# A graph convolution on one core: SP fetches 44 gathered rows in a turn in place of 32

## The reference, cut to what matters

```python
h = relu(layernorm(x))                       # x: 12500 nodes x 128
xp = h @ lin1_w
C = 0.5 * (cos(edge_weight * PI / CUTOFF) + 1.0)
W = (ssp(edge_attr @ mlp_w1 + mlp_b1) @ mlp_w2 + mlp_b2) * C[:, None]   # 212500 edges, 50 -> 128
msg = xp[src] * W                            # gather of 212500 rows of xp
agg = segment_sum(msg, dst, num_segments=12500)      # dst is sorted
out = x + (ssp(agg @ lin2_w + lin2_b) @ lin_w + lin_b)
```

## Time and profile before

| | |
|---|---|
| median of 3 runs | 2022.07 us (2021.86 to 2024.72) |
| the profiled execution | 2022.45 us, its span 2020.7 us |
| busy: PE, DVE, ACT, POOL | 66%, 52%, 39%, 75% of the span |
| POOL's gathers in the main part | 1542, 944 ns each |
| rows fetched one by one | 3092 by SP, 3840 by ACT |
| granted TensorE clock, mean | 0.819 |

### The profile page before, as it was taken

One profiled execution on the slowest core, in us unless ns is written; L12 is line 12 of the kernel. 1 busy time (PEld: TensorE's weight loads), 2 busy tenths in 40 slices (PEclk: granted clock), 3 DMA queues, 4 the chain that ended last, 5 costly groups with the idle time before them and its releaser, 6 DMA issues.

```text
span 2020.7 us, 48993 instructions
## 1 busy us (share of the span) xinstructions
PE 1341.8 (66%) x12880; PEld 1108.7 (55%) x12881; DVE 1048.1 (52%) x3153; ACT 792.7 (39%) x925; POOL 1517.5 (75%) x1611
## 2 busy tenths in 40 slices
PE   5577667776776777676666666666666666666666
PEld 5465556655555556555555555555555555555454
DVE  8664655555545555555544444444544444445454
ACT  5764333333434443433343333333333334333332
POOL 7777777777777777777777777777777777777775
PEclk9887888888888878888787888778877878887887
DMA  9633343333343344334333233333333333333322
GB/s 320 247 94 92 89 97 88 98 98 92 92 99 97 88 97 99 87 93 102 87 88 97 77 97 90 84 98 81 92 94 80 98 86 88 97 88 87 96 76 51
DMA packets 114579, 202.33 MB, mean 100 GB/s; under 512 B 36409, under 2 KB 69917, under 8 KB 114173
## 3 DMA queue, kind: packets, MB, share of 16 engines
q0 software_dynamic: 51392, 105.35, 21.6%
q1 hardware_dynamic: 55228, 91.86, 14.7%
q10 hardware_dynamic: 7680, 1.98, 0.7%
HBM read 186.25 MB, written 12.80 MB: 99 GB/s over the span
## 4 chain that ended last, share of the span: by engine, by line
POOL 38%; ACTq 19%; issue 18%; ACT 16%; PE 4%; DVE 3%; DMA 1%; DVEq 0%; SPq 0%; POOLq 0%
POOL XG L460 38%; ACTq L576 17%; ACT TB L593 5%; ACT TB L587 4%; ACT TB L590 4%; ACTq L565 1%; PE PW L878 1%; ACT XG L482 1%; DMA XG<-xp_scratch,IX 1%; PE PA L897 1%; DVE XG L776 1%; DVE TB L651 1%; DVE SCR L630 1%; PE PX L824 1%; PE PX L862 0%
## 5 line engine op out<-in xcount | busy, mean ns | idle before, releaser
L460 POOL DMA_INDIRECT XG<-xp_scratch,IX x1542 | 1455.6, 944 | 470.6 <-issue 463.0
L776 DVE SCALAR_TENSOR_TENSOR XG<-PW,CC,XG 128x128 f32<-128x128 f32 x1602 | 453.1, 344 | 435.3 <-DMA XG<-xp_scratch,IX 399.6
L587 ACT ACTIVATE TB<-PX 128x1024 f32<-128x1024 f32 x208 | 212.8, 1023 | 1039.8 <-PE PX L862 532.9
L875 PE MATMUL PW<-BPB,ones 128*128 128x512 bf16 x415 | 183.7, 443 | 563.3 <-DVE XG L776 558.8
L878 PEld LDWEIGHTS PW<-W,TB 128*128 128x128 f32 x3314 | 545.9, 234 | 20.0
L878 PE MATMUL PW<-W,TB 128*128 128x128 f32 x3314 | 548.9, 320 | 0.0
L731 DVE SCALAR_TENSOR_TENSOR TB<-PX,TB 128x1024 f32<-128x1024 f32 x208 | 254.2, 1222 | 347.1 <-ACT TB L593 336.5
L875 PEld LDWEIGHTS PW<-BPB,ones 128*128 128x128 bf16 x415 | 41.2, 99 | 674.2 <-issue 670.2
L897 PE MATMUL PA<-OH,XG 128*64 128x64 f32 x6408 | 296.1, 259 | 0.0
L897 PEld LDWEIGHTS PA<-OH,XG 128*64 128x64 f32 x6408 | 265.4, 171 | 31.3 <-issue 18.4
L862 PE MATMUL PX<-AT,W 51*128 51x256 f32 x1662 | 258.2, 432 | 2.6 <-ACT XG L482 2.6
(11 more groups left out here) (107 smaller groups left out, 538.1 us busy)
## 6 DMA issues: line engine op xcount, KB each, us to landing
HA<-xp_scratch ACTq DMA_DIRECT2D x3840, 0.5 KB
AT<-attr_b SPq DMA_DIRECT2D x104, 512.0 KB
HT<-xp_scratch SPq DMA_DIRECT2D x3092, 0.5 KB
XG<-xp_scratch,IX POOLq DMA_INDIRECT x1542, 2.7
AG<-zero SPq DMA_DIRECT2D x1, 6400.0 KB, 21.6
xp_scratch<-XG SPq DMA_DIRECT2D x24, 256.0 KB
XR<-x SPq DMA_DIRECT2D x24, 256.0 KB
out<-XR SPq DMA_DIRECT2D x24, 256.0 KB, 3.8
```

Source lines behind the costliest of these rows:

```text
L460: e.indirect_dma_start(XG[q % XG_N][0:p, k * D:(k + 1) * D], None, xp, bass.IndirectOffsetOnAxis(ap=IX[0:p, t0 + k:t0 + k + 1], axis=0)).t ...
L587: e.activation(T, PXP[pair % 2][:, :], ACT.Abs).then_inc(s_ab, 1)
L776: ins = e.scalar_tensor_tensor(out=G, in0=weights(q)[0:p, k * D:(k + 1) * D], scalar=CC[0:p, t0 + k:t0 + k + 1], in1=G, op0=ALU.mult, op1= ...
L875: e.matmul(P[0:p, 0:n * D], ones[:, 0:p], BP[0][:, 0:n * D], start=True, stop=False, skip_group_check=True)
```

## The change

SP's turn gets 44 rows in place of 32. `HQ` has 34 quads in place of 25, spaced 12 quads, at times 8: 30, 42, 54, ..., 126, 138, 146, 158, ..., 402, 414. Tile `j`'s last row comes in turn ceil(128(j + 1)/44) - 1 and its quad is 18 + 4 ceil(128(j + 1)/44). POOL skips the first tile of each of these quads, so it has 9 gathers less. The row numbers lie in a table `SI` by turns (101 x 44 in place of 25 x 128), a turn is two halves, and a half loads 22 numbers with one instruction and then issues 22 rows; a wait for a free `HT` buffer stands between rows where a tile begins. The last row, number 4243, falls into turn 96 as its twentieth. ACT's rows, the buffers and the rest of SP's queue are as before.

```diff
-ROWS = 32
-NH = (NCH - 3 - 2) * ROWS // TILE
-HQ = {18 + (j + 1) * TILE * CHQ // ROWS: j for j in range(NH) if 18 + (j + 1) * TILE * CHQ // ROWS < NQ - 2}
+ROWS = 44
+TURNS = NCH - 3
+HQ = {18 + -(-(j + 1) * TILE // ROWS) * CHQ: j for j in range((TURNS - 2) * ROWS // TILE)}
+HQ = {q: j for q, j in HQ.items() if q < NQ - 2}
...
-        SI = sb("SI", [NH, TILE], i32)
+        SI = sb("SI", [TURNS, ROWS], i32)
...
-            def fetch(a, b):
-                n = a
-                while n < b:
-                    j, p = n // TILE, n % TILE
-                    m = min(8 - n % 8, b - n)
-                    if p == 0 and j >= HT_N:
-                        e.wait_ge(s_sc, HAND[j - HT_N] + 1)
+            def fetch(turn):
+
+                for h in range(0, ROWS, ROWS // 2):
+                    n0 = turn * ROWS + h
+                    if n0 >= END:
+                        return
                     _, at = nc.values_load_multi_w_load_instructions(
-                        SI[j:j + 1, p:p + m], engines=[mybir.EngineType.SP], min_val=0, max_val=ROW * (NODES - 1),
+                        SI[turn:turn + 1, h:h + ROWS // 2], engines=[mybir.EngineType.SP], min_val=0, max_val=ROW * (NODES - 1),
                     skip_runtime_bounds_check_because="src holds node numbers, which are below NODES")
-                    for i, v in enumerate(at):
-                        e.dma_start(HT[j % HT_N][p + i:p + i + 1, :].bitcast(u8), row(v)).then_inc(s_r[j % HT_N], 16)
-                    n += m
+                    for n, v in zip(range(n0, END), at):
+                        j, p = n // TILE, n % TILE
+                        if p == 0 and j >= HT_N:
+                            e.wait_ge(s_sc, HAND[j - HT_N] + 1)
+                        e.dma_start(HT[j % HT_N][p:p + 1, :].bitcast(u8), row(v)).then_inc(s_r[j % HT_N], 16)
...
-                fetch(min(END, (k - AT_N) * ROWS), min(END, (k - AT_N + 1) * ROWS))
+                fetch(k - AT_N)
...
-        "src_h": _np.ascontiguousarray(tiles(g["src"]).T[[quad(q)[0] for q in HAND]]),
+        "src_h": turns(tiles(g["src"]).T[[quad(q)[0] for q in HAND]], TURNS, ROWS),
```

## The result

| | before | after |
|---|---|---|
| median | 2023.39 us (4 runs, three of them those of the section on the time before) | 2340.71 us (2336.47 to 2343.56, 4 runs) |
| ratio, 95% interval | | 1.156 (1.154 to 1.159) |
| span of the profiled execution | 2020.7 us | 2339.5 us |
| POOL's gathers | 1542 | 1533 |

The forecast was 2010.9 us within a range of 2008.5 to 2037; the change costs 317 us. POOL has its 9 gathers less, and it does not matter.

What follows compares the result with a forecast made beforehand. POOL, gathering without a pause, was taken to bound the kernel: 9 gathers fewer at 1.249 us save 11.2 us, so span 2020.7 - 11.2 = 2009.5 us, plus 1.4 for the median, 2010.9 us; range 2008.5 to 2037.

Steps and rivals of the forecast that it cites:

- SP's part: what a turn costs after: SP's queue: twelve rows more add 3.96 us, loads take off 0.17, restarts 0.14; a turn goes from 14.56 to 18.2 us.
- rival (a): SP's queue becomes the bound because its turn is dearer than worked out, from 18.34 us a turn; chance 0.29 past break-even.
- strictly by number: Upper bound for SP's load of 22: 22/8 x 0.792 = 2.18 us, giving 2127 us; chance 0.03.
- The turn of 24 us: SP's turn if registers cost about 200 ns each, two loads of 22 making 8.8 us; set aside for the trace's prices.
- The two slopes: Register loads' price for each further number: 0.049 us on SP (one to eight), 0.053 on ACT (one to twenty).
- The sum over turns: SP's path to the end: 249.3 us plus 96 turns; at 18.2 us a turn it ends at 1996.5 us.
- POOL's 9 gathers: POOL loses 9 gathers at 1.249 us each, 11.2 us, all on the path that sets the end.
- The floor: POOL working without a pause sets the end: span 2009.5 us, median 2010.9 us; chance 0.57.
- Twelve rows at 0.33 us: SP's twelve additional single rows in a turn, each 0.33 us, together 3.96 us more.
- The dear first row behind a load: SP's first row after each load of 22 might cost 0.2 us more; turn 18.6 us, 2035 us, chance 0.12.
- The load of `x` rows: In SP's queue behind the longer turn; its sum comes out some 5 us earlier than the chunk's, so it decides nothing.
- Rival (c): The 9 gathers bring nothing because POOL fills its ring instead; alone it would give 2021 us; chance 0.01.

## Why the prediction was wrong

**The step that failed** is "SP's part: what a turn costs after", and in it the load of 22 numbers, taken at 1.50 us within 1.48 to 2.18. It measured 1.88 us at the start of the table's row and 4.88 at byte 88. Both loads together were 6.76 us a turn in place of 3.00. The mechanism by which that decides was forecast, as rival (a), with a chance of 0.29: SP's queue becomes the bound, chunks come late. Only its upper end, 2127 us, was too low, since the bound "strictly by number" took the price per number from loads of eight at multiples of 32 bytes (0.099 us), not from one that begins off a multiple of 16 (0.22 us). The turn of 24 us that the prediction set aside would have made 249.3 + 96 x 24 = 2553 us, for only one of the two loads is that dear.

**What the trace of before could have said.** The two slopes rested on counts of 1, 8 and 20, and on starts at bytes 0, 32, 64, ... for SP and 0 and 80 for ACT. No load of it began off a multiple of 16 bytes or ended off one, save those of one number. I looked at the count as the only thing that changes; the change also moved the start to a place unlike all others. The Trainium skill, "Runtime: NRT & Kernel Launch", section "Instruction fetch mechanics", gives about 200 ns for each register even in bulk. I set it aside because the page speaks of loads from HBM, and eight numbers took 0.79 us. From SBUF it fits the load off the 16 bytes (0.22 us a number) and each number of a rest (0.21); for loads of whole fours that begin on them it is two to three times too high (0.79 / 8 = 0.10, 1.97 / 28 = 0.07).

**The sum over turns** comes out near, by two errors that cancel in part. With the turn of the first four, 249.3 + 96 x 21.72 = 2334 us; the span is 2339.5. But the mean turn was 22.21 us, 0.22 of it stores and `x` loads, so 21.99: 0.27 more in each, 26 us in all. And the stretch behind turn 96 was taken at 102 us and took 80: its nine pairs went at 6.1 us, not 8.51. ACT's last row was issued at 2244.7 us and POOL's last gather at 2252.5, before this stretch begins (2259.3); which of the two frees the pairs, no run took apart. PE's first matrices of the last pair began at 2317.5, 22.0 us before the end (21.6 forecast).

```profile
2262.87 2.08 PE L864 MATMUL PX<-AT,W 51*128 51x256 f32 x8 [9.48 <-DMA AT<-attr_b]
...
2317.49 1.13 PE L864 MATMUL PX<-AT,W 51*128 51x20 f32 x6
```

**Point by point.** POOL's 9 gathers: right, 1533 of 944 ns; the 11.2 us were lost in its waits. The floor is real: the kernels with 36 and 40 rows, and the one with ACT's share cut, sit within 1.3 us of theirs. Twelve rows at 0.33 us: right in the kernel after (0.332), wrong near the limit of 4.4 rows a us. This is a second term put at nothing: rows of SP and ACT in one DMA engine. With aligned loads it would still have been 2064 us, outside the range. The dear first row behind a load: it stayed at 0.27 us behind 22 numbers, this risk was none. The load of `x` rows "decides nothing": DVE waited 200 us for it, 21 times, in an SP-bound kernel in which the chunks are as late, and with loads of 24 and 20 it stood on the chain that ended last; no run took it apart from the chunks. Rival (c), a full ring of POOL: it came, 282.6 us of waits, as a consequence of (a), as the forecast put it.

## What to carry to other kernels

A load of many registers from a table was priced here by where it begins and by its count's rest, 0.25 us for four numbers against 0.21 for one of a rest; cut tables so that every load begins at a multiple of four numbers and has a multiple of four. Before work is moved to a queue with reserve, sum that queue's turn, multiply its error by the number of turns (96 here: 0.1 us is 10 us), and ask of each instruction whether its start and size are like one that the trace has priced. And count what all queues send to the same place: two queues of single-row transfers, each within its own pace, were over a limit here that neither shows, and they delayed a share of every bulk load. Look at when the packets start, not only at when they are issued.

## What the runs showed of the hardware

- TENSOR_LOAD on SP from SBUF: 1.23 us for 16 numbers, 0.25 more for each four, 0.21 for each of a rest of one to three; 4.88 us for 22 numbers at six of eight starts, 1.92 at the two that are multiples of 16 bytes.
- Single rows of 512 bytes issued by SP and ACT together passed at 4.34 to 4.40 a us on average over 96 turns, in five kernels with different turns, beside this kernel's gathers and chunk loads. Near that limit an ACT row's packet started 5 to 12 us after its issue (median) in place of 1.2, and SP's rows were issued up to 0.35 us apart in place of 0.332.
- Near it, a sixteenth of every 512 KB chunk load (8 of 128 packets) started from 10.5 us after the issue on (median), the others within 3.3, and those packets took turns with the rows: all single rows go through one DMA engine (the kernel with loads of 24 and 20).
- In two sessions the unchanged kernel took 2827 and 2832 us, against 2023 in the others, with SP and ACT often halting at the same moments for 0.7 us. The chip of the first has the same number, 3, as that of a later session with 2023 us, so it is not shown that the chip is the cause. What halts them stays open.
